# A planned transformer kernel: identity matmuls put in by planned array work, and a reordered opening with weight casts on GpSimd

## The reference, cut to what matters

```
x = x + 0.5 * ffn(ln(x))          # L0: w1, w2 (128 -> 512), h1, h2 (512 -> 512), w3 (512 -> 128)
x = x + attn0(ln(x))              # linear attention without softmax
x = x + 0.5 * ffn(ln(x))          # the same weights
x = x + 0.5 * moe(ln(x))          # L1: 8 low-rank experts, top 2 by the first row of each batch
x = x + attention(ln(x))          # 16 heads of 8, rotary, causal, softmax
x = x + 0.5 * moe(ln(x))

ffn: h = silu(x @ w1 * s) * (x @ w2 * s); h = gelu(h @ h1 * s); h = gelu(h @ h2 * s); h @ w3 * s
```

## Time and profile before

| what | value |
|---|---|
| three runs | 640.28, 642.38, 642.96 us; median 642.38 |
| the profiled execution, its own time | 645.81 us |
| its span, first to last instruction | 644.0 us (1.8 us lie outside) |
| mean granted TensorE clock | 0.984 of full speed |
| busy share of the span | PE 94%, DVE 74%, ACT 75%, POOL 36% |
| PE busy, 32 to 400 us | 363.05 of 368.00 us |
| PE busy, 436 to 510.3 us | 66.76 of 74.30 us |

### The profile page before, as it was taken

The page is one execution under the profiler, slowest core; times in us unless marked ns, Lnnn a source line. Parts: engine busy times, 40 slices in busy tenths (PEclk is TensorE's granted clock), DMA queues, the critical chain, the costliest instruction groups (busy, mean ns, idle before and its releaser), DMA issues.

```text
span 644.0 us, 17311 instructions
## 1 busy us (share of the span) xinstructions
PE 607.3 (94%) x6902; PEld 472.0 (73%) x6902; DVE 476.0 (74%) x1298; ACT 479.9 (75%) x832; POOL 233.1 (36%) x354
## 2 busy tenths in 40 slices
PE   4899999999999999999999999998898999999997
PEld 3677878888887887888877887665565667766675
DVE  6667566765766778656777668898899787788964
ACT  5799778787788787887878776745778466778792
POOL 1402303312312526403337346756654542331032
PEclk9999999999999999999999999999999896899999
DMA  9300000000000001100003003413444423223002
GB/s 295 110 2 1 0 1 2 1 2 1 1 1 1 1 2 49 50 2 2 0 7 92 1 22 119 135 47 132 147 131 128 143 77 114 88 90 101 23 13 60
DMA packets 41230, 35.24 MB, mean 55 GB/s; under 512 B 2952, under 2 KB 37032, under 8 KB 41148
## 3 DMA queue, kind: packets, MB, share of 16 engines
q1 hardware_dynamic: 41148, 34.12, 16.8%
HBM read 19.17 MB, written 14.68 MB: 53 GB/s over the span
## 4 chain that ended last, share of the span: by engine, by line
PE 63%; DVE 14%; ACT 11%; issue 6%; POOL 2%; DMA 2%; SPq 1%; POOLq 0%; DVEq 0%; ACTq 0%
PE PSA L1009 20%; PE PSA L1013 19%; PE PSA L1248 5%; DVE MX L1438 3%; PE PSA L1028 3%; DVE G L1316 3%; ACT PB L1587 2%; ACT PSA L1492 2%; DVE RA L1431 2%; PE PSA L1236 2%; PE PSA L1227 1%; ACT G L1488 1%; PE PSA L1172 1%; PE PSA L1192 1%; PE PSA L1165 1%
## 5 line engine op out<-in xcount | busy, mean ns | idle before, releaser
L1009 PE MATMUL PSA<-ah,WH 128*128 128x512 f32 x320 | 130.5, 408 | 2.4 <-DVE al L1321 1.5
L1013 PE MATMUL PSA<-al,WH 128*128 128x512 f32 x320 | 125.1, 391 | 0.0
L1492 ACT ACTIVATE PSA<-PSA,SC 128x512 f32<-128x512 f32 x128 | 84.6, 661 | 50.8 <-PE PSA L1013 50.3
L1438 DVE TENSOR_REDUCE MX<-PSA 128x10 f32<-128x640 f32 x128 | 101.2, 815 | 17.7 <-PE PSA L1199 17.3
L1009 PE MATMUL PSA<-bh,WH 128*128 128x512 f32 x256 | 105.7, 413 | 3.1 <-DVE G L1316 3.1
L1013 PE MATMUL PSA<-bl,WH 128*128 128x512 f32 x256 | 100.2, 391 | 0.0
L1587 ACT ACTIVATE PB<-PSA 128x640 f32<-128x640 f32 x128 | 84.8, 703 | 20.3 <-PE PSA L1236 19.1
L1321 DVE TENSOR_TENSOR al<-PSA,ah 128x512 fp32r<-128x512 f32 x64 | 44.0, 688 | 56.5 <-ACT ah L1499 56.4
L1614 POOL TENSOR_SCALAR VE<-MV 128x4 f32<-128x4 f32 x46 | 11.2, 244 | 205.4 <-DVE MV L1291 205.4
L1009 PEld LDWEIGHTS PSA<-ah,WH 128*128 128x128 f32 x320 | 60.2, 188 | 17.6 <-DVE al L1321 3.8
L1013 PEld LDWEIGHTS PSA<-al,WH 128*128 128x128 f32 x320 | 60.2, 188 | 11.8 <-issue 1.0
(11 more groups left out here) (168 smaller groups left out, 1281.6 us busy)
## 6 DMA issues: line engine op xcount, KB each, us to landing
KQ<-dk SPq DMA_DIRECT2D x32, 192.0 KB
KQ<-dq SPq DMA_DIRECT2D x32, 192.0 KB
dk<-CB SPq DMA_DIRECT2D x16, 192.0 KB, 2.5
dq<-CB SPq DMA_DIRECT2D x16, 192.0 KB, 2.6
X<-in_x SPq DMA_DIRECT2D x8, 256.0 KB, 6.8
dk<-CB SPq DMA_DIRECT2D x16, 128.0 KB, 1.9
dq<-CB SPq DMA_DIRECT2D x16, 128.0 KB, 2.7
W<-in_w SPq DMA_DIRECT2D x3, 512.0 KB, 5.7
```

What stands on the lines that cost most here:

```text
L1009: e.matmul(o, WH[:, col:col + 128], hi, start=first, stop=False)
L1013: return e.matmul(o, WH[:, col:col + 128], low, start=False, stop=last)
L1438: e.tensor_reduce(MX[:, u % 2, :, :].rearrange("p t (l g) -> p l t g", l=2)[:, :, :, g], PSA[:, b:b + 2, 0:320].rearrange("p l (t k) -> p ...
L1492: e.activation(bank(b), bank(b), ACT.Gelu, scale=SC[:, k:k + 1]).then_inc(a_gelu, 1)
```

## The change

Opening: VectorE fills the tile MK with ones, TensorE issues 15 matmuls 128x512 on it at once and 3 more behind the first transposes, and ScalarE makes one Silu of one column before all else. `cast_a` and `cast_v` of the parts 3 and 4 and their `low` move to GpSimd (`cast_g`, `low_g`). Only scan 0 stays in `begin`; the others, the flag and `mark` become a job (`mark`) that is added when the first chunk's `up`, `silu`, `mul` and `split` steps are put. So all four `up` of the first chunk, and the `hid` steps that are put before `mark`, have three matmuls for each product. The first chunk's first hidden layer is put two output tiles at a time. The second stream's first chunk may be put once the plan's TensorE clock is at 14.0. The small load SC is issued earlier, and `masks` waits for the first `up` and `silu`.

Fillers: `fill` takes 0.85 of a gap less 0.06, from one matmul up, and has a second form "h" of four 64x64 matmuls with 256 columns. New is `hold`: once one stream has ended, it adds up the planned array work (WORK) of the last stretch before a TensorE step of the tile kinds f and h, and where that is under a set share it puts up to 8 fillers (4 of form h) ahead of the step, gap or not.

Plan: some durations in TAKES are changed, and SHIFT has 79 entries in place of 64, nearly all with other values. Two waits of `half_norm` and `half_xt` now name their source step's number.

```diff
-    "up_first": [("P", 2.7, 2.85)], "up": [("P", 0.92, 1.07)], "silu": [("A", 0.57, 0.68)], "mul": [("V", 0.66, 0.75)],
+    "up_first": [("P", 1.36, 1.52)], "hid_first": [("P", 1.36, 1.52)], "down_first": [("P", 1.36, 1.52)], "up": [("P", 0.92, 1.07)], "silu": [("A", 0.57, 0.68)], "mul": [("V", 0.66, 0.75)],
...
-    "expert": [("P", 0.42, 0.6), ("V", 0.33, 0.41)],
-    "qk": [("P", 0.95, 1.02), ("V", 1.9, 2.05)], "turned": [("G", 1.23, 1.27)],
+    "expert": [("P", 0.47, 0.66), ("V", 0.33, 0.41)],
+    "qk": [("P", 0.88, 1.06), ("V", 1.9, 2.05)], "turned": [("G", 1.23, 1.27)],
...
-COMES = {"stat": [3.5], "cast_v": [5.6, 12.6], "cast_a": [7.1, 8.5, 10.6]}
+COMES = {"stat": [3.5, 14.6], "cast_v": [5.3], "cast_a": [7.9, 8.9], "cast_g": [10.7, 12.7]}
...
-FILLED = 0.65
+HOLD = (3.4, 0.42)
+FILLED = 0.85
+SPARE = 0.06
+OPEN = 14.0
+WARM = (15, 3)
...
+    ("after", 0, 2): 0.24, ("after", 0, 3): 0.24, ("after", 0, 4): 0.28, ("after", 1, 1): -0.39,
...
-        if name == "up" and not self.opened:
-            late = "up_first"
+        if name in ("up", "hid", "down") and not self.opened:
+            late = name + "_first"
...
-                self.fill(s0)
-                self.idle_from = s0 + us
+                self.fill(s0, kind)
+                s0 = self.hold(s0, kind)
+                self.worked.append((s0, s0 + us, WORK.get(name, 0.0)))
+                self.idle_from, self.last = s0 + us, kind
...
+    def keep(self, form, n, a, each, banks):
+        if n <= 0:
+            return
+        self.note("P", a, a + each * n, "keep" + form)
+        self.worked.append((a, a + each * n, n * {"h": 0.107, "f": 0.053, "w": 0.107}[form]))
+        k = self.count.get("keep", 0)
+        self.count["keep"] = k + 1
+        self.steps.insert(-1, Step("keep", k, x=n, b=min(banks), b2=max(banks), kind=form,
+                                   emptied=sum((self.bank[b] for b in banks), [])))
+
+    def fill(self, t, kind):
+
+        free = sorted((self.left(f), b) for b, f in enumerate(self.bank) if f)
         if not free or not self.opened:
             return
 
-        each = 0.06 if self.count.get("masks") else 0.23
-        b = min(free, key=lambda b: self.left(free[b]))
-        n = int((t - max(self.idle_from, self.left(free[b]) + 0.06) - 0.15) * FILLED / each)
-        if n > 1:
-            self.note("P", max(self.idle_from, self.left(free[b]) + 0.06), max(self.idle_from, self.left(free[b]) + 0.06) + each * n, "keep")
-            k = self.count.get("keep", 0)
-            self.count["keep"] = k + 1
-            self.steps.insert(-1, Step("keep", k, x=n, b=b, kind="w" if each > 0.1 else "", emptied=free[b]))
+        h = self.last == "h" and self.bank[6] is not None and self.bank[7] is not None
+        h = h and self.left(self.bank[6] + self.bank[7]) <= max(self.idle_from, free[0][0] + 0.1)
+        if h:
+            free = [(self.left(self.bank[6] + self.bank[7]), 6), (0.0, 7)]
+        form = "h" if h else "f" if self.count.get("masks") else "w"
+        each = {"h": 0.125, "f": 0.06, "w": 0.23}[form]
+        own = form if h else "f"
+        a = max(self.idle_from + 0.094 * (self.last != own), free[0][0] + 0.06)
+        n = int((t - a - 0.094 * (kind != own) - SPARE) * FILLED / each)
+        if n > (not h):
+            self.keep(form, n, a, each, [b for _, b in free[:1 + h]])
+
+    def hold(self, t, kind):
+
+        if len(self.dead) < 1 or kind not in "fh":
+            return t
+        done = 0.0
+        for a, z, work in reversed(self.worked):
+            if a < t - HOLD[0] - 4.0:
+                break
+            done += work * max(0.0, min(z, t) - max(a, t - HOLD[0])) / (z - a)
+        free = [b for _, b in sorted((self.left(f), b) for b, f in enumerate(self.bank) if f and self.left(f) + 0.06 < t)]
+        if kind == "h":
+            free = [b for b in free if b > 5]
+        short = HOLD[0] * HOLD[1] - done
+        if short <= 0.05 or len(free) <= (kind == "h"):
+            return t
+        each, work = (0.125, 0.107) if kind == "h" else (0.06, 0.053)
+        n = min(int(short / work + 0.99), int(0.5 / each))
+        self.keep(kind, n, t, each, free[:2 if kind == "h" else 1])
+        return t + each * n
 
...
-        self.put("cast_a", j=3)
         self.put("scan", j=0)
-        self.put("cast_v", j=4)
         for j in (3, 4):
-            self.put("low", j=j)
-            self.put("scan", j=j - 2)
-        self.put("scan", j=3)
-        self.last_scan = self.put("scan", j=4)
+            self.put("cast_g", j=j)
+        self.put("low_g", j=3)
+
+    def mark(self):
+
+        scans = []
+        for j in range(1, 5):
+            scans.append(self.put("scan", j=j))
+            yield from self.until(scans[-1].done - 3.5)
+        yield from self.until(scans[-1].done - 4.0)
+        st = self.put("second_parts", src=scans[-1])
+        b, free = yield from self.sr.get(self)
+        yield from self.until(st.done - 1.3)
+        st = self.put("flag", b=b, emptied=free, src=st)
+        self.sr.free[b] = [st]
+        yield from self.until(st.done - 0.1)
+        self.put("mark", src=st)
+        self.opened = True
 
     def feed(self, s, box):
         p, c = box["ffn"]
-        while not self.opened:
+        while not self.opened and self.clock["P"] < OPEN:
...
-            parts, last, early = [], None, []
-            if first:
-
-                for j in range(3):
-                    b, free = yield from self.single()
-                    b2, free2 = yield from self.single()
-                    g, gfree = yield from self.gr.get(self)
-                    early.append((self.put("up", c=c, j=j, s=s, b=b, b2=b2, emptied=free, emptied2=free2, src=xt),
-                                  b, b2, g, gfree))
-                st = self.put("second_parts", src=self.last_scan)
-                b, free = yield from self.sr.get(self)
-                st = self.put("flag", b=b, emptied=free, src=st)
-                self.sr.free[b] = [st]
-                self.put("mark", src=st)
-                self.opened = True
+            parts, last = [], None
             for j in range(4):
-                if early:
-                    mm, b, b2, g, gfree = early.pop(0)
-                else:
-                    b, free = yield from self.single()
-                    b2, free2 = yield from self.single()
-                    g, gfree = yield from self.gr.get(self)
-                    mm = self.put("up", c=c, j=j, s=s, b=b, b2=b2, emptied=free, emptied2=free2, src=xt)
+                b, free = yield from self.single()
+                b2, free2 = yield from self.single()
+                g, gfree = yield from self.gr.get(self)
+                mm = self.put("up", c=c, j=j, s=s, b=b, b2=b2, emptied=free, emptied2=free2, src=xt)
...
+            if first:
+                self.put("low_g", j=4)
+                self.add(0, self.mark())
             box = self.next_feed(s)
             for lay in range(2):
                 nxt = []
-                for j in range(4):
+                for j in range(0, 4, 2) if first and not lay else ():
+                    got = []
+                    for x in (0, 2):
+                        for k in (j, j + 1):
+                            if not x:
+                                got.append((yield from self.single()))
+                            b, free = got[k - j]
+                            yield from self.until(parts[x + 1].done)
+                            mm = self.put("hid", c=c, j=k, x=x, g=lay, s=s, b=b, emptied=free, src=parts)
+                            yield
+                            if x:
+                                ge = self.put("gelu", c=c, j=k, g=lay, b=b, src=mm)
+                                nxt.append(self.put("split", c=c, j=k, g=1 + lay, s=s, b=b, src=ge))
+                                self.bank[b] = [nxt[-1]]
+                for j in range(len(nxt), 4):
...
-            w.wait_ge(v_wh, 1 + (part > 3))
-            w.wait_ge(a_wh, min(part, 3))
+            w.wait_ge(v_wh, 1)
+            w.wait_ge(a_wh, min(part, 2))
+            w.wait_ge(g_wh, part - 2)
...
-                    w.wait_ge(v_wl, NEEDED[part])
+                    w.wait_ge(v_wl, min(NEEDED[part], 3))
+                    w.wait_ge(g_wl, NEEDED[part] - 3)
...
+                    if st.name == "xtf" and not n:
+                        warm(e, WARM[1])
...
-                        ID = IDN if early else IDB
-                        e.matmul(PSA[:, b, 0:128], ID[:, :], ID[:, :], start=True, stop=True)
+                        if st.kind == "h":
+                            for x in range(2):
+                                for h in range(2):
+                                    e.matmul(PSA[64 * x:64 * x + 64, (st.b, st.b2)[h], 0:256], IM[64 * h:64 * h + 64, 0, 0:64],
+                                             IM[64 * h:64 * h + 64, :, :].rearrange("p k m -> p (k m)"), start=True, stop=True)
+                        else:
```

(28 more changed lines are left out.)

53 lines of the change are left out of this document (30 added, 23 removed), and 16 rows, old and new, of the table TAKES.

## The result

The changed kernel takes 648.41 us (median of 14 runs, 647.13 to 651.99), the kernel before 642.20 us (14 runs, 638.05 to 646.95): ratio 1.0101, 95% interval 1.0078 to 1.0123. It is slower by 6.2 us where 632 us was forecast, and outside the range of 624 to 643. Its profiled execution took 649.31 us, span 647.5 us, granted clock 0.990. Three executions in the rounds behind this document that took 956 to 1441 us, two of the kernel before and one of `before_warm`, belong to a slow state and are in none of the ratios.

The account below looks back on a forecast made before the run. Bound by ScalarE in the opening, TensorE from 32 to 400 us, and no single engine from 436 us, with TensorE's low clock on the path; 645.8 - 5.5 - 6.5 + 1.5 = 635.3, scaled to 632 us, range 624 to 643.

Parts of the forecast that it names:

- The opening (-5.5): Up to 32 us: earlier silu, warm TensorE and moved casts let the feed-forward run ahead; 5.5 us gained, bounds 2 to 8.
- Who waits is scan 4, thus the flag and `mark`: Opening: the lows on GpSimd delay only scan 4, moving `mark` from about 18 to about 25 us, and the second stream's norm.
- TensorE idle on VectorE's or GpSimd's norm: Sign that the forecast is wrong: TensorE idle waiting for a norm between 16 and 26 us.
- The balance: Opening: time without useful TensorE work falls from 21.9 to 16.1 us, with both streams feeding TensorE from 25 us.
- opening gain lost: Rival: GpSimd queue, scans between gelus and third terms leave 1 us of the opening's gain; 636 us, chance 0.10.
- The clock (-6.5): Attention stage: fillers remove two falls to 1.2 GHz, 20.5 us together, gaining 6.5 us; bounds 0 to 9.9.
- The limit by the engine that is next to bind: Attention stage: at VectorE's earlier busy share, its work during the clock falls takes 14.0 us, giving the 6.5 us gain.
- The clock stays low: Rival: fillers go where the plan sees little work, and the attention stage's clock falls remain or move; 638 us, chance 0.18.
- The fillers (+1.5): Attention stage: fillers put ahead of work that could start cost 1.5 us on the path, some 21 fillers; bounds 0 to 20.
- while the plan's gaps are real: `fill`'s larger share of gaps (0.85 for 0.65) stays hidden if the gaps exist; otherwise its cost is within the 1.5 us.
- The order (0, bounded by 5): From about 32 us on, new TAKES and SHIFT change every engine's order; counted 0, bounded by 5 us either way.
- fillers on the path: Slower rival: `hold` stands ahead of TensorE steps that something waits for, 40 fillings costing 20 us; 650 us, chance 0.12.

Follow-up runs that it names:

- before_warm: The kernel before with only the early warm matmuls and the early Silu added: 644.27 us, ratio 1.0041.
- port: Computes nothing, copies x to the output, runs VectorE and GpSimd instructions alone or together: four VectorE subtractions took 2.50 us alone, 5.18 beside one GpSimd subtraction.
- low_on_vector: The changed kernel, same order, with the two lows of parts 3 and 4 on VectorE in place of GpSimd: 644.99 us, ratio 1.0046.
- low_in_pieces: The changed kernel, same order, with each low on GpSimd cut into five operations of 256 columns: 645.05 us, ratio 1.0051.
- the repaired kernel: Another name for `low_on_vector`, the changed kernel with its two lows on VectorE: 644.99 us, ratio 1.0046.
- the six draws: Six kernels with orders not fitted to their timeline: the two halves, and the kernel before and `low_on_vector`, each with SHIFT emptied or its signs turned: 654 to 680 us.
- the two halves: The kernel before with the changed TAKES, SHIFT, `fill` and `hold`: 658.32 us; `low_on_vector` with TAKES, SHIFT and `fill` of before, no `hold`: 660.97 us.

## Why the prediction was wrong

**The opening (-5.5).** Three of its readings held: no table load stands ahead of the scans, neither behind the early Silu at 10.24 us nor behind the silus at 23.71 (the Trainium skill, "ScalarE: Activation LUTs", Table sets, had it so, and the timeline now shows it), the first silu came at 11.28 us, even before the forecast 13.3, and the fourth `up` was done by 15.9. The first hidden product was due near 17.2 and came at 18.14. The step that failed is the GpSimd part. It priced the lows right (3.3 us each forecast, 3.1 measured), the casts too low (1.3 forecast, 1.95 measured), and then charged them to GpSimd's own queue: "Who waits is scan 4, thus the flag and `mark`", and the second stream's norm. Who waited first was VectorE, held up by the GpSimd instruction itself. `port` shows the mechanism, `low_on_vector` and `low_in_pieces` price it at 3.4 us in the whole. The prediction named "TensorE idle on VectorE's or GpSimd's norm" as a sign against it, but not the lows as the reason.

Through that stop the clock fell, TensorE ran 6.8 us at 1.2 GHz, and the flag's matmul came at 30.6 us instead of "about 25": the sums' reduction was started at 28.43, and the flag's matmul then stood, as the queue is in order, in TensorE's queue behind products of three terms. 24 weight-low matmuls were issued for six before, 18 x 0.23 = 4.1 us.

Even repaired, the opening gained 1.4 us at 32 us, 24 products for 21, not 5.5, and 0 at the end of the feed-forward: its last matmul comes at 429.9 us for 429.6. The balance counted what TensorE can do from the first hidden product on and took both streams as running from 25 us. The second came at 28.4. Rival "opening gain lost" had the place and two of the reasons (one GpSimd queue, third terms up to a late flag), with 1 us left of the gain; it was nearer than the forecast, and still too kind at the end.

**The clock (-6.5).** The step that failed is the size of what could be won. The sum took 20.5 us at half clock from one profiled execution as the kernel's habit. Over 98 executions before has a median of 11.5 us, and its profiled one, clock 0.984 and 645.81 us, was near the worst. At 0.34 us a us the 11.5 are worth 3.9 us. The limit by the engine that is next to bind, 6.5 of 20.5 or 0.32 a us, agrees with that rate. The changed kernel won none of it (13.0 us at half clock), since the new fall in the opening ate what the attention stage gave; repaired it won 6.4 us of half clock, 2.2 us of time at that rate and less at its own slope of 0.10. "The clock stays low" was wrong as a rival: the falls of 510 to 551 us went.

**The fillers (+1.5).** `hold` was taken as what places them; it placed 8 of 414 matmuls, and the larger share in `fill` placed the rest. That share was said to be hidden "while the plan's gaps are real". By the estimate of the table the identities of the repaired kernel cost 4.6 us in all, 0.9 more than before's. So the term may have been of the right size, 1.5 against an estimated 0.9; neither of the two reasons for it held.

**The order (0, bounded by 5).** This bound was wrong by the most. What "the attention stage's slack suggests" says nothing about it: changes of priorities alone moved the kernel by 12 to 38 us. The changed kernel's own offsets bring it to within 2.8 us of before with the lows repaired; by the table's estimate that is 4.9 us of the rest less 2.2 of the clock, and 4.0 of the 4.9 are there without any identities. That these 4.0 are a somewhat worse fit of the offsets fits with the six draws, but it isn't shown: the two halves could not be timed apart, because each half alone loses the fit. What costs the 4.0 stays open: the order, the added terms and scans of the opening and the casts that stay on GpSimd are all in them.

**The sum**, from before: +3.4 lows on GpSimd (with the fall of the clock that they bring), which is measured, and for the other 2.8 measured, by the estimate of the table, +4.0 order and opening together, +0.9 fillers, -2.2 clock: +6.1, for 6.2 measured. That it closes is no proof, since the terms of the table are differences of the same medians. The rival on the slower side, "fillers on the path" at 650 us, was near in time and wrong in cause.

## What to carry to other kernels

Before work is moved to GpSimd, list what VectorE does meanwhile with two SBUF inputs, and its casts from SBUF: such an instruction can wait for a whole GpSimd instruction, so cut the GpSimd work into pieces or leave it where it is. Take the time at a low clock from many executions, not from the profiled one, before pricing its cure, and give filler matmuls a cost wherever the step behind them is waited for (0.03 to 0.05 us of 0.07 here). In a kernel whose queues follow a fitted order, a change of the opening or of a duration is also a new order, and that term can be larger than all others: fit it again before judging the change, and don't price it at nothing.

## What the runs showed of the hardware that was not expected

- A VectorE subtraction of 512 columns with both inputs in SBUF takes 0.69 us, and 3.19 and 2.73 us when a GpSimd subtraction of 1280 columns runs; a cast of 512 columns takes 0.42 us, and 3.10 when it is caught by one. Beside GpSimd casts of 1280 columns two of VectorE's lows took 3.41 us, and 2.35 in the opening of before, which had nothing on GpSimd.
- Over 98 executions of the kernel before, a us at 1.2 GHz goes with 0.34 us of time. In other kernels of this case the slope is 0.10 to 0.31, and why isn't shown.
- TensorE's clock fell behind two different pasts: 6.22 of 6.83 us busy with small matmuls, and in the changed opening 2.32 of the 6.07 us from 14.53 to 20.6, idle for the last 1.6 us.
